# Two-layer block kernel: first half of the attention outputs turned and projected inside the last block

## The chip, the cores and the metric

One core of one Trainium2 chip. A core has TensorE (matmul; "PE" in the profile, its weight loads "PEld"), VectorE ("DVE"), ScalarE ("ACT"), GpSimd ("POOL") and SyncE ("SP"), which issues the transfers. Each engine runs its own instructions in the order of the program and meets the others by semaphores. The metric is the time of one execution on the device, in microseconds (us).

## What is computed

A block of four stages over 1024 tokens of width 256, each stage added to x behind a layer norm with learned shifts, scales and gates. Stage 1 is a linear attention, stage 2 a feed-forward part with 4-bit weights, stage 3 a masked softmax attention, stage 4 a feed-forward part of width 1024 whose gate has a low-rank term made from a second softmax attention. Cut to what the change touches:

```python
# stage 3: x = x + ga * _L1_attn_ref(h, ...)
att = jnp.where(causal, jnp.einsum('bhqd,bhkd->bhqk', q, k) / scale, -jnp.inf)   # 16 heads of width 16
y = jnp.einsum('bhqk,bhkd->bhqd', jax.nn.softmax(att, axis=-1), v)
y = jnp.einsum('bte,fe->btf', y.transpose(0, 2, 1, 3).reshape(b, t, e), Wo) + bo
# stage 4: x = x + gb * _L1_ffn_ref(h, ...)
attn = _attention(_rmsnorm(hidden_states, ln1_w), Wq, Wk, Wv, Wo)   # the same kind of attention
mod = MOD_SCALE * jnp.tanh(attn @ A)                                # A: 256 x 16
h = _rmsnorm(residual, ln2_w)
gate_pre = h @ W_in_base.T + mod * (h @ A) @ B
mlp_out = jax.nn.silu(gate_pre) * (h @ W_up_base.T) @ W_down.T
return residual + mlp_out
```

## The kernel before

The program is written out engine by engine, with counting semaphores; there is no scheduler at build time except one planner for the attention. x stands in SBUF with tokens on the partitions (8 tiles of 128 tokens). Projections want the channels on the partitions, so TensorE turns tiles of 128 x 128 (a "transpose" is a matmul against the identity `ident`), four to a PSUM bank; the eight banks hold 512 float32 values per partition each. "Half 0" is the first 512 tokens, "half 1" the other 512.

The softmax attention is run twice, `attention(0)` for stage 3 and `attention(1)` for stage 4 ("layer 0" and "layer 1" below). It works in 8 blocks: blocks 0 to 3 are four groups of heads over the queries of half 0, blocks 4 to 7 the same groups over the queries of half 1. For each block TensorE makes the scores once for their row maxima ("max", L750, taken by VectorE at L1303), and then again as transposed scores ("score", L776 with the mask L779) in steps of 128 keys; ScalarE takes the exponential of each pair of score banks (L972); TensorE multiplies with the values ("value", L790) into bank 3. At a block's end ScalarE copies bank 3 to SBUF ("copy", L990), TensorE turns it ("out", L799), and VectorE divides by the sum (L1322, L1324) into `att`, which has tokens on the partitions. A planner, `attention_order`, puts these pieces into one list `ORDER`, and TensorE, ScalarE and VectorE each walk through it. Steps 40 to 47 belong to block 7; step 44 is the first of its four masked steps. Block 3's sums, the last of half 0, are divided long before block 7 starts, block 6's during its first steps.

Behind `attention(0)` TensorE turns `att` (`attention_transposes`, L499, 16 transposes), ScalarE copies the four banks to `hT` (`attention_out`, L910), TensorE multiplies with the output weights (`out_projection`, L508, four units u of half and output channels, two matmuls each over kc, float32), ScalarE scales each unit (`projected`, L920), TensorE turns the result back in four quarters v (`update`, L521), VectorE adds each to x (L1226) and goes on with the norm of stage 4.

Behind `attention(1)` TensorE turns `att` (16 transposes, ScalarE's copies at L912), makes h times A for both halves (low-rank input; 12 matmuls, L463 to L465), then the attention outputs times the product of Wo and A (low-rank output; 4 float32 matmuls, L865). ScalarE takes the tanh (L1092), VectorE multiplies the two (three operations a half, from L1518). The feed-forward part `mlp(1)` begins with h times the first weights. Its weights are loaded by SyncE once all scores are done; ScalarE makes their high parts (`mlp_weights_hi`, L1002) and VectorE the low parts (`mlp_weights_lo`, L1368). GpSimd has the subtraction L1621 in each of its units.

## Time and profile before

| | us |
|---|---|
| median of 3 runs | 710.5 |
| lowest, highest | 709.95, 713.21 |
| the profiled execution, its own time | 709.6 |
| its span, first to last instruction | 707.9 |

| engine | busy us | share of the span |
|---|---|---|
| TensorE, matmuls | 654.1 | 92% |
| TensorE, weight loads | 407.0 | 58% |
| VectorE | 457.4 | 65% |
| ScalarE | 334.6 | 47% |
| GpSimd | 150.3 | 21% |

Matmuls overlap in the records (each row runs until its result is out), so a busy TensorE is not one at its peak, and the start of the next row tells more of the pace than a duration. A float32 matmul leaves two records. A row "x4" stands for four instructions in a stretch. In square brackets stands the idle time of the engine before the row and what ended it. The layer 0 attention runs from about 280 to 428 us, its output stage to 440, the layer 1 attention from about 470 to 619, and the feed-forward part from 629 to 701.

### The profile page before, as it was taken

Reading aid. Unit: us, or ns where it says so; the run is one execution under the profiler, and the core shown is the slowest. Engines: PE = TensorE matmul, PEld = TensorE weight load, DVE = VectorE, ACT = ScalarE, POOL = GpSimd, SP = SyncE. Lnnn points to the kernel's source line nnn. Section 1 sums busy time; section 2 is a strip of 40 time slices with the busy share of each in tenths; the row PEclk is TensorE's granted clock in tenths of the full one; section 3 lists DMA queues with packets and bytes.
Section 4 is the critical chain, followed back from the end, with each engine's and each line's share of the span. In section 5 each row is a group of like instructions: output and inputs, shape, how many; then the busy total and the mean of one; then the engine's idle time right before and its main releaser. Section 6 shows DMA issues by size and latency. Waiting matters only on the chain.

```text
span 707.9 us, 10654 instructions
## 1 busy us (share of the span) xinstructions
PE 654.1 (92%) x3959; PEld 407.0 (58%) x3965; DVE 457.4 (65%) x970; ACT 334.6 (47%) x531; POOL 150.3 (21%) x194
## 2 busy tenths in 40 slices
PE   4999989999999879799999998898899999999996
PEld 3666657777777746355444435484454444368884
DVE  5658787777777288778888602548688887242223
ACT  5325243333333423345566684562464657843332
POOL 3001224555555701310000000031100001002331
PEclk9999799999999999989999999999999999999999
DMA  8602410000000003566000000075540000050001
GB/s 270 219 0 91 120 53 0 24 22 23 1 0 1 0 1 91 132 183 135 2 2 2 2 1 1 0 177 149 122 93 2 2 2 3 16 164 1 0 1 59
DMA packets 36415, 38.34 MB, mean 54 GB/s; under 512 B 4034, under 2 KB 35292, under 8 KB 36108
## 3 DMA queue, kind: packets, MB, share of 16 engines
q1 hardware_dynamic: 36364, 37.67, 19.5%
q8 instruction: 31, 0.51, 0.3%
q14 instruction: 20, 0.16, 0.1%
HBM read 30.11 MB, written 7.34 MB: 53 GB/s over the span
## 4 chain that ended last, share of the span: by engine, by line
PE 50%; issue 22%; POOL 11%; DVE 9%; ACT 3%; SPq 2%; DMA 1%; POOLq 0%; DVEq 0%; ACTq 0%
POOL it_lo L1621 9%; PE psum L790 9%; PE psum L750 8%; PE psum L776 7%; PE psum L463 4%; PE psum L464 3%; PE psum L465 3%; POOL wd L1600 2%; DVE m L1303 2%; PE psum L508 2%; PE psum L779 2%; PE psum L753 2%; PE psum L579 2%; DVE mx L1303 1%; DVE x L1226 1%
## 5 line engine op out<-in xcount | busy, mean ns | idle before, releaser
L972 ACT ACTIVATE pt<-psum 128x1024 f32<-128x1024 f32 (+1 forms) x192 | 148.2, 811 | 94.4 <-PE psum L779 62.8
L1303 DVE TENSOR_REDUCE mx<-psum 128x1 f32<-128x512 f32 (+3 forms) x216 | 132.4, 664 | 16.4 <-PE psum L750 8.4
L750 PE MATMUL psum<-kr,qr 96*128 96x512 bf16 (+3 forms) x384 | 110.7, 338 | 10.3 <-DVE m L1303 5.2
L776 PE MATMUL psum<-qr,kr 99*128 99x512 bf16 (+3 forms) x384 | 99.2, 332 | 1.5 <-ACT pt L972 1.3
L1621 POOL TENSOR_TENSOR it_lo<-it,it_hi 128x512 fp32r<-128x512 f32 x48 | 67.2, 1401 | 146.9 <-ACT it_hi L1016 145.3
L790 PE MATMUL psum<-pt,vp 128*32 128x512 f32 (+3 forms) x768 | 82.1, 500 | 0.0
L750 PEld LDWEIGHTS psum<-kr,qr 96*128 96x128 bf16 x384 | 36.9, 100 | 73.7 <-DVE mx L1303 29.4
L463 PE MATMUL psum<-h_hi,wf_hi 128*128 128x512 f32 x192 | 75.5, 393 | 0.1
L1016 ACT CAST it_hi<-it 128x512 fp32r<-128x512 f32 x48 | 29.9, 622 | 95.6 <-DVE it L1380 95.6
L464 PE MATMUL psum<-h_lo,wf_hi 128*128 128x512 f32 x192 | 74.9, 390 | 0.0
L465 PE MATMUL psum<-h_hi,wf_lo 128*128 128x512 f32 x192 | 74.9, 390 | 0.0
L1303 DVE TENSOR_REDUCE m<-psum 128x1 f32<-128x384 f32 (+3 forms) x88 | 50.8, 634 | 21.7 <-PE psum L753 21.4
L1380 DVE TENSOR_TENSOR it<-psum,gl 128x512 f32<-128x512 f32 x48 | 32.8, 684 | 43.1 <-PE psum L465 39.6
L776 PEld LDWEIGHTS psum<-qr,kr 99*128 99x128 bf16 x384 | 35.8, 99 | 41.5 <-ACT pt L972 23.0
L779 PE MATMUL psum<-identb,tri 128*128 128x128 bf16 x256 | 51.3, 223 | 0.0
L753 PE MATMUL psum<-tri,identb 128*128 128x128 bf16 x256 | 51.2, 228 | 0.0
L1651 POOL TENSOR_SCALAR m<-m 128x16 bf16<-128x16 f32 x16 | 4.0, 253 | 220.6 <-DVE m L1309 153.9
L463 PE MATMUL psum<-it_hi,wf_hi 128*128 128x512 f32 x96 | 39.5, 411 | 7.2 <-POOL it_lo L1621 7.2
L463 PEld LDWEIGHTS psum<-h_hi,wf_hi 128*128 128x128 f32 x192 | 36.1, 188 | 8.5 <-issue 0.8
L464 PEld LDWEIGHTS psum<-h_lo,wf_hi 128*128 128x128 f32 x192 | 36.1, 188 | 7.7 <-issue 0.2
L465 PEld LDWEIGHTS psum<-h_hi,wf_lo 128*128 128x128 f32 x192 | 36.1, 188 | 7.7
L1012 ACT ACTIVATE gl<-psum 128x512 f32<-128x512 f32 x48 | 28.6, 596 | 24.3 <-PE psum L542 16.4
(201 smaller groups left out, 1082.7 us busy)
## 6 DMA issues: line engine op xcount, KB each, us to landing
parts_scratch<-parts SPq DMA_DIRECT2D x12, 384.0 KB, 3.9
qr<-parts_scratch SPq DMA_DIRECT2D x16, 192.0 KB, 3.1
kr<-parts_scratch SPq DMA_DIRECT2D x16, 192.0 KB, 3.7
qr<-parts_scratch SPq DMA_DIRECT2D x16, 128.0 KB, 3.2
kr<-parts_scratch SPq DMA_DIRECT2D x16, 128.0 KB, 3.6
wmod<-in_L_wmod SPq DMA_DIRECT2D x1, 1536.0 KB, 6.1
parts_scratch<-qr SPq DMA_DIRECT2D x4, 384.0 KB, 4.7
x<-in_L_attn_x SPq DMA_DIRECT2D x2, 512.0 KB, 4.0
```

Source lines behind the costliest of these rows:

```text
L463: pe.matmul(dst, st_hi, mv_hi, start=first, stop=False)
L464: pe.matmul(dst, st_hi, mv_lo, start=False, stop=False)
L465: return pe.matmul(dst, st_lo, mv_hi, start=False, stop=last)
L750: m = pe.matmul(b, qr[0:PARTS_ROWS, c, h, (qt - 4 * c) * P:(qt - 4 * c + 1) * P], kr[0:PARTS_ROWS, ch, h, 0:w], start=True, stop=not diag)
L753: m = pe.matmul(b[:, w - P:w], identb[:, :], tri[:, :], start=False, stop=True)
L776: m = pe.matmul(bank[4 + 2 * at[0] + j][:, 0:w], kr[0:PARTS_ROWS + 3, kt // 4, h, (kt % 4) * P:(kt % 4 + 1) * P], qr[0:PARTS_ROWS + 3, c, ...
L779: m = pe.matmul(bank[4 + 2 * at[0] + j][:, 0:P], tri[:, :], identb[:, :], start=False, stop=True)
L790: m = pe.matmul(bank[3][32 * j:32 * j + 32, q0 - c * HALF:q0 - c * HALF + w], vp[:, kt, 4 * gp + j, :], pt[:, (n + j // 2) % 4, j % 2, 0:w ...
L972: act.activation(pt[:, n % 4, :, 0:w], psum[:, b:b + 2, 0:w], ACT.Exp, scale=0.25).then_inc(S["ex"], 1)
L1303: dve.tensor_reduce(dst, bank[at[0]][:, 0:k * w].rearrange("p (k w) -> p k w", k=k), AX, ALU.max).then_inc(S["p1_mx"], 1)
L1380: dve.tensor_tensor(it[:, N % 2, :], bank[5][:, :], gl[:, N % 2, :], ALU.mult).then_inc(S["it_s"], 1)
L1621: pool.tensor_tensor(it_lo[:, N % 2, :], it[:, N % 2, :], it_hi[:, N % 2, :].bitcast(F32), ALU.subtract).then_inc(S["it_l"], 1)
```

## The change

In both layers, the eight transposes of half 0 move from behind the attention into block 7, behind the second score pair of step 44 (`AHEAD = 44`), and ScalarE's two copies of them behind the exponentials of that step. They use banks 0 and 1; half 1 stays behind the attention and uses banks 6 and 7.

In layer 0 the output projection is split. The first matmul of unit 0 stands ahead of block 7's "out" transposes, where TensorE waits for ScalarE's copy of the sums; the second stands behind them, where it waits for VectorE. Then come the transposes of half 1, units 1 and 2, the transposes of x for quarters 0 and 1, unit 3, and quarters 2 and 3.

In layer 1 the low-rank output of half 0 stands ahead of the "out" transposes, the low-rank input of half 0 behind them, then the transposes of half 1, the low-rank input and the low-rank output of half 1. ScalarE takes the tanh of half 0 first, VectorE has the three operations of half 0 ahead of the low parts of the first weights. No instruction is added or taken away on any engine.

```diff
+AHEAD = 44
+        def att_bank(k, half, dt):
+            return ((6, 7, 0, 1) if k == 0 else (0, 1, 6, 7))[2 * half + dt]
+        def wo_bank(k, u):
+            return ((2, 3, 4, 5) if k == 0 else (0, 1, 4, 5))[u]
...
+            def out_projection(k, u, kcs=range(KC)):
+                half, dt = divmod(u, 2)
+                pe.wait_ge(S["at_e"], 4 * k + 2 * half + 2)
+                for kc in kcs:
+                    m = pe.matmul(bank[wo_bank(k, u)][:, :], woT[k][:, kc, dt * P:(dt + 1) * P],
+                                  attT[k][:, kc, half * HALF:(half + 1) * HALF],
+                                  start=kc == 0, stop=kc == KC - 1)
+                if kc == KC - 1:
                     m.then_inc(S["wo_m"], 1)
...
+            def low_rank_out(half):
+                pe.wait_ge(S["at_e"], 8 + 2 * half + 2)
+                for kc in range(KC):
+                    m = pe.matmul(bank[(4, 2)[half]][0:96, :], woa[:, kc, :],
+                                  attT[2][:, kc, half * HALF:(half + 1) * HALF], start=kc == 0, stop=kc == KC - 1)
+                m.then_inc(S["z_m"], 1)
+
+            def low_rank_in(half):
+                pe.wait_ge(S["h_ok"], 2 * half + 2)
...
                         m.then_inc(S["s2"], 1)
+                        if i == AHEAD and at[0] == 1:
+                            pe.wait_ge(S["att_w"], 8 * (l + 1) + 7)
+                            attention_transposes(l + 1, 0)
...
                     elif what == "out":
                         n = 8 * l + i
+                        if n == 7:
+                            out_projection(1, 0, (0,))
+                        elif n == 15:
+                            low_rank_out(0)
                         pe.wait_ge(S["ob"], n + 1)
...
             attention(0)
-            attention_transposes(1)
-            out_projection(1)
-            update(2)
+            out_projection(1, 0, (1,))
+            attention_transposes(1, 1)
+            out_projection(1, 1)
+            out_projection(1, 2)
+            update(2, 0, 2)
+            out_projection(1, 3)
+            update(2, 2, 4)
...
             attention(1)
-            attention_transposes(2)
-            pe.wait_ge(S["at_e"], 12)
             pe.wait_ge(S["ab"], 2)
...
+            low_rank_in(0)
+            attention_transposes(2, 1)
+            low_rank_in(1)
+            low_rank_out(1)
+            pe.wait_ge(S["z_ok"], 1)
             pe.wait_ge(S["bst"], 2)
             mlp(1)
...
+                        if i == AHEAD and at[0] == 1:
+                            attention_out(l + 1, 0)
...
+            def low_rank_tanh(half):
+                act.wait_ge(S["z_m"], half + 1)
+                act.activation(t1[0:96, half, :], bank[(4, 2)[half]][0:96, :], ACT.Tanh).then_inc(S["z_ok"], 1)
...
             attention(0)
-            attention_out(1)
-            projected(1)
+            projected(1, 0, 1)
+            attention_out(1, 1)
+            projected(1, 1, 4)
...
             attention(1)
-            attention_out(2)
+            low_rank_tanh(0)
+            attention_out(2, 1)
             mlp_weights_hi(1, 0)
-            for half in range(2):
-                act.wait_ge(S["z_m"], half + 1)
-                act.activation(t1[0:96, half, :], bank[2 + half][0:96, :], ACT.Tanh).then_inc(S["z_ok"], 1)
+            low_rank_tanh(1)
             mlp(1, ACT.Silu)
...
             attention(1)
-            mlp_weights_lo(1, 0)
 
             for half in range(2):
+                if half:
+                    mlp_weights_lo(1, 0)
                 dve.wait_ge(S["ha_m"], half + 1)
```

TensorE in layer 0, from the last value products (`pt`, `vp`) of block 7 to the fillers ahead of the norm (`spin`), before; `t` is the copy of the sums, `xn` with `ident` the transposes of `att` and then of the projected outputs, `hT,woT` the output projection:

```order
L790 MATMUL psum<-pt,vp 32x256 x4
L790 MATMUL psum<-pt,vp 32x128 x4
L799 MATMUL psum<-ident,t 128x128 x4
L499 MATMUL psum<-ident,xn 128x128 x16
L508 MATMUL psum<-hT,woT 128x512 x8
L521 MATMUL psum<-ident,xn 128x128 x16
L812 MATMUL psum<-a_rep,raw 128x96 x4
L480 MATMUL psum<-spin,identb 128x512 x18
```

and now:

```order
L818 MATMUL psum<-pt,vp 32x256 x4
L818 MATMUL psum<-pt,vp 32x128 x4
L515 MATMUL psum<-hT,woT 128x512
L831 MATMUL psum<-ident,t 128x128 x4
L515 MATMUL psum<-hT,woT 128x512
L507 MATMUL psum<-ident,xn 128x128 x8
L515 MATMUL psum<-hT,woT 128x512 x4
L529 MATMUL psum<-ident,xn 128x128 x8
L515 MATMUL psum<-hT,woT 128x512 x2
L529 MATMUL psum<-ident,xn 128x128 x8
L848 MATMUL psum<-a_rep,raw 128x96 x4
L489 MATMUL psum<-spin,identb 128x512 x18
```

Eight transposes are gone from here, a matmul of the projection stands on either side of the transposes of the sums, and the turning back is in two parts. The eight stand in step 44, ahead of the value product of step 43:

```order
L801 MATMUL psum<-qr,kr 128x512
L804 MATMUL psum<-identb,tri 128x128
L507 MATMUL psum<-ident,xn 128x128 x8
L818 MATMUL psum<-pt,vp 32x512 x4
L801 MATMUL psum<-qr,kr 128x384
```

where the scores (`qr,kr`) and mask (`tri`) of step 44 were followed by the value product at once. ScalarE in layer 1, from step 44's exponentials (`pt`) to the first of the feed-forward part (`gl`), before, with the semaphores that each row waits for:

```order
L972 ACTIVATE pt<-psum 128x1024 [waits pv,s2] x2
L972 ACTIVATE pt<-psum 128x2x384 [waits pv,s2] x2
L972 ACTIVATE pt<-psum 128x2x256 [waits pv,s2] x2
L972 ACTIVATE pt<-psum 128x2x128 [waits pv,s2] x2
L990 COPY t<-psum 128x512 [waits ot,pv]
L912 COPY attT<-psum 128x512 [waits att_t] x4
L1002 CAST wf_hi<-nat 128x768 [waits nat0,fdn]
L1092 ACTIVATE t<-psum 96x512 [waits z_m] x2
```

and now:

```order
L996 ACTIVATE pt<-psum 128x1024 [waits pv,s2] x2
L936 COPY attT<-psum 128x512 [waits att_t] x2
L996 ACTIVATE pt<-psum 128x2x384 [waits pv,s2] x2
L996 ACTIVATE pt<-psum 128x2x256 [waits pv,s2] x2
L996 ACTIVATE pt<-psum 128x2x128 [waits pv,s2] x2
L1016 COPY t<-psum 128x512 [waits ot,pv]
L1032 ACTIVATE t<-psum 96x512 [waits z_m]
L936 COPY attT<-psum 128x512 [waits att_t] x2
L1028 CAST wf_hi<-nat 128x768 [waits nat0,fdn]
L1032 ACTIVATE t<-psum 96x512 [waits z_m]
```

Two of the four copies stand ahead of step 45's exponentials, and one tanh ahead of the other two copies.

## Rows read from the trace of the kernel before

**Rows 1.** The page, the chain that ended last, shares of the span by engine.

```profile
PE 50%; issue 22%; POOL 11%; DVE 9%; ACT 3%; SPq 2%; DMA 1%; POOLq 0%; DVEq 0%; ACTq 0%
```

**Rows 2.** Timeline, layer 0, steps 44 and 45: start, us, engine, line, operation, [idle before].

```profile
419.33 1.94 ACT L972 ACTIVATE pt<-psum 128x1024 f32<-128x1024 f32 x2 [0.38 <-PE psum L779]
...
420.77 0.10 PEld L776 LDWEIGHTS psum<-qr,kr 99*128 99x128 bf16 x1 [0.84 <-ACT pt L972]
...
421.32 0.10 PEld L776 LDWEIGHTS psum<-qr,kr 99*128 99x128 bf16 x1 [0.21 <-ACT pt L972]
...
421.43 1.51 ACT L972 ACTIVATE pt<-psum 128x768 f32<-128x768 f32 x2 [0.16 <-PE psum L779]
```

**Rows 3.** Timeline, layer 0, from the last value product to the norm's transposes.

```profile
425.59 0.16 PEld L790 LDWEIGHTS psum<-pt,vp 128*32 128x32 f32 x8 [0.43 <-ACT pt L972]
...
426.72 0.42 PEld L799 LDWEIGHTS psum<-ident,t 128*128 128x128 f32 x4 [0.97 <-ACT t L990]
...
428.25 1.73 PEld L499 LDWEIGHTS psum<-ident,xn 128*128 128x128 f32 x16 [1.11 <-issue]
...
428.94 2.42 ACT L910 ACTIVATE hT<-psum,vec 128x512 f32<-128x512 f32 x4 [2.27 <-PE psum L499]
...
430.26 7.13 PE L508 MATMUL psum<-hT,woT 128*128 128x512 f32 x16
...
432.34 0.78 ACT L920 ACTIVATE xn<-psum,gbo,gate 128x512 f32<-128x512 f32 x1 [0.98 <-PE psum L508]
...
437.43 0.78 ACT L920 ACTIVATE xn<-psum,gbo,gate 128x512 f32<-128x512 f32 x1 [0.94 <-PE psum L508]
...
439.81 0.67 DVE L1226 TENSOR_TENSOR x<-psum,x 128x512 f32<-128x512 f32 x1
...
445.74 1.09 PE L472 MATMUL psum<-ident,xn 128*128 128x128 f32 x8 [0.40 <-DVE xn L1134]
```

**Rows 4.** Timeline, layer 1, from the last value product to the feed-forward part.

```profile
617.70 0.16 PEld L790 LDWEIGHTS psum<-pt,vp 128*32 128x32 f32 x8 [0.43 <-ACT pt L972]
...
618.83 0.42 PEld L799 LDWEIGHTS psum<-ident,t 128*128 128x128 f32 x4 [0.97 <-ACT t L990]
...
620.36 1.73 PEld L499 LDWEIGHTS psum<-ident,xn 128*128 128x128 f32 x16 [1.11 <-issue]
...
621.05 2.05 ACT L912 COPY attT<-psum 128x512 f32<-128x512 f32 x4 [2.27 <-PE psum L499]
...
623.16 0.16 PEld L463 LDWEIGHTS psum<-h_hi,a_hi 128*96 128x96 f32 x1 [1.07 <-ACT attT L912]
...
625.79 0.39 PE L465 MATMUL psum<-h_hi,a_lo 128*96 128x512 f32 x1
...
629.45 0.19 PEld L464 LDWEIGHTS psum<-h_lo,wf_hi 128*128 128x128 f32 x1 [0.24 <-issue]
```

**Rows 5.** Timeline, layer 1, the split of the weights and the low-rank product.

```profile
622.97 0.87 ACT L1002 CAST wf_hi<-nat 128x768 fp32r<-128x768 f32 x1
...
623.96 0.96 DVE L1368 TENSOR_TENSOR wf_lo<-nat,wf_hi 128x768 fp32r<-128x768 f32 x1 [3.72 <-ACT wf_hi L1002]
...
628.63 0.68 DVE L1518 SCALAR_TENSOR_TENSOR t<-t,psum 96x512 f32<-96x512 f32 x1 [3.71 <-ACT t L1092]
...
629.81 0.68 DVE L1524 TENSOR_TENSOR m_hi<-t,m_hi 32x512 fp32r<-32x512 f32 x1
...
634.13 1.29 POOL L1621 TENSOR_TENSOR it_lo<-it,it_hi 128x512 fp32r<-128x512 f32 x1 [38.26 <-ACT it_hi L1016]
...
634.92 1.32 DVE L1368 TENSOR_TENSOR wf_lo<-nat,wf_hi 128x768 fp32r<-128x768 f32 x1 [1.52 <-ACT wf_hi L1002]
```

**Rows 6.** Busy time by stretch: from:to, length, engines' busy (count), PEclk granted, DMA.

```profile
300.00:304.00 4.00, 4.00 (x21) 2.24 (x20) 3.97 (x7) 0.00 (x0) 0.33 (x2) 0.50 0.60 145
...
500.00:504.00 4.00, 4.00 (x33) 2.19 (x31) 2.19 (x4) 1.19 (x2) 0.00 (x0) 0.67 0.90 177
...
638.00:696.00 58.00, 58.00 (x256) 47.85 (x255) 16.25 (x19) 21.46 (x33) 17.61 (x14) 1.00 0.00 1
```

More of the change, by code:

```diff
@@ L492, in token_major, with attention_transposes, update @@
                 return m
-            def attention_transposes(k):
-                for u in range(4):
-                    half, dt = divmod(u, 2)
-                    pe.wait_ge(S["att_w"], 8 * k + (4 * half + 4 if k == 0 else 8))
+            def attention_transposes(k, half):
+                for dt in range(KC):
+                    pe.wait_ge(S["att_w"], 8 * k + (4 * half + 4 if k == 0 or half == 0 else 8))
                     for j in range(4):
-                        m = pe.transpose(bank[(6, 7, 0, 1)[u]][:, j * P:(j + 1) * P],
+                        m = pe.transpose(bank[att_bank(k, half, dt)][:, j * P:(j + 1) * P],
                                          att[:, 4 * half + j, dt * P:(dt + 1) * P], ident[:, :])
                     m.then_inc(S["att_t"], 1)
-            def out_projection(k):
-                for u in range(4):
-                    half, dt = divmod(u, 2)
-                    pe.wait_ge(S["at_e"], 4 * k + 2 * half + 2)
-                    for kc in range(KC):
-                        m = pe.matmul(bank[2 + u][:, :], woT[k][:, kc, dt * P:(dt + 1) * P],
-                                      attT[k][:, kc, half * HALF:(half + 1) * HALF],
-                                      start=kc == 0, stop=kc == KC - 1)
+            def out_projection(k, u, kcs=range(KC)):
[6 more added lines that the diff above has]
+                if kc == KC - 1:
                     m.then_inc(S["wo_m"], 1)
-            def update(r):
-                for v in range(4):
+            def update(r, first=0, last=4):
+                for v in range(first, last):
                     pe.wait_ge(S["ysem"], 4 * r + 2 * (v // 2) + 2)
@@ L669, in _ @@
             pe.wait_ge(S["mod_cp"], 3)
-            attention_transposes(0)
+            attention_transposes(0, 0)
+            attention_transposes(0, 1)
             pe.wait_ge(S["ca"], 8)
             pe.wait_ge(S["wt_hi"], 5)
-            out_projection(0)
+            for u in range(4):
+                out_projection(0, u)
             update(0)
@@ L716, in _ @@
             spread_transposes(1)
+            def low_rank_out(half):
[6 more added lines that the diff above has]
+                pe.wait_ge(S["h_ok"], 2 * half + 2)
+                tok = slice(half * HALF, (half + 1) * HALF)
+                for kc in range(KC):
+                    m = mm3(bank[half][0:96, :], a_hi[:, kc, :], a_lo[:, kc, :], h_hi[:, kc, tok], h_lo[:, kc, tok],
+                            kc == 0, kc == KC - 1)
+                m.then_inc(S["ha_m"], 1)
             def attention(l):
@@ L901, in layer_norm_mod, with attention_out @@
                                    bias=mod[:, l, 6 * second + dt:6 * second + dt + 1]).then_inc(S["ln_f"], 1)
[L903 to L907 removed]
+            def attention_out(k, half):
+                for dt in range(KC):
+                    act.wait_ge(S["att_t"], 4 * k + 2 * half + dt + 1)
+                    b, dst = bank[att_bank(k, half, dt)], attT[k][:, dt, half * HALF:(half + 1) * HALF]
                     if k == 1:
@@ L913, in attention_out, with projected @@
                     q.then_inc(S["at_e"], 1)
-            def projected(k):
+            def projected(k, first=0, last=4):
                 act.wait_ge(S["mod_ok"], k + 2)
-                for u in range(4):
+                for u in range(first, last):
                     half, dt = divmod(u, 2)
                     act.wait_ge(S["wo_m"], 4 * k + u + 1)
-                    act.activation(y[:, dt, half * HALF:(half + 1) * HALF], bank[2 + u][:, :], ACT.Identity,
+                    act.activation(y[:, dt, half * HALF:(half + 1) * HALF], bank[wo_bank(k, u)][:, :], ACT.Identity,
                                    scale=gate[:, k, 4 + dt:5 + dt], bias=gbo[:, k, dt:dt + 1]).then_inc(S["ysem"], 1)
@@ L1087, in _ @@
             attention(1)
-            attention_out(2)
+            low_rank_tanh(0)
+            attention_out(2, 1)
             mlp_weights_hi(1, 0)
-            for half in range(2):
-                act.wait_ge(S["z_m"], half + 1)
-                act.activation(t1[0:96, half, :], bank[2 + half][0:96, :], ACT.Tanh).then_inc(S["z_ok"], 1)
+            low_rank_tanh(1)
             mlp(1, ACT.Silu)
```

20 lines of the change are left out of this document (2 added, 18 removed).

## Prediction

> **What bounds the kernel now.** I read three views: the chain of work that ended last, then the timeline around the two places that the change touches (the end of each masked attention), then the busy time and granted clock by stretches. The chain [rows 1] gives TensorE half of the span, and 22% to "issue", time in which nothing shown released the engine. So the kernel is mostly TensorE in program order, and what can be won is TensorE time on the path, or a wait of TensorE that ends last. The timeline at the end of layer 0's attention [rows 3] shows two such waits in a row: 0.9 us for ScalarE's copy of the last sums and 1.1 us for VectorE to divide them. Layer 1 has the same two, and then 1.07 us for ScalarE's copy of the turned outputs [rows 4]. Behind layer 1's end comes the feed-forward part, where TensorE is busy 58.00 of 58.00 us [rows 6], so that time won ahead of it reaches the end of the kernel. Behind layer 0's end comes the norm, a chain of VectorE and ScalarE for which TensorE waits (the last row of [rows 3]): there a gain counts from the moment at which VectorE gets its last additions of x.
>
> **Cost inside the last block, both layers.** Behind score step 44 stand 8 transposes more. 16 of them load in 1.73 us [rows 3], so 8 take 0.86 on TensorE. Queued behind them are the value product of step 43 and the scores of step 45; ScalarE's exponentials wait for these. ScalarE gets two copies: 4 took 2.42 in layer 0 [rows 3] and 2.05 in layer 1 [rows 4], so 1.21 and 1.03, queued ahead of the exponentials of step 45. Who is held? In layer 0 the two exponentials of step 44 run from 419.33 to 421.27 [rows 2], the copies then to 422.48. TensorE, which began the scores of step 45 at 420.77 and released an exponential 0.66 later [rows 2], begins at 421.63 and releases it at 422.29. It starts at 422.48 instead of 421.43, 1.05 later; but TensorE had been held by ScalarE once here (0.21) and ScalarE by TensorE (0.16), and these take back a part. Followed step by step with the durations of the trace, the last value product starts 0.8 us later in layer 0, and a little less in layer 1, whose copies are shorter. I take **0.8 and 0.8**. Bounds: 0.65 each if the 0.21 is all slack, and 2.07 and 1.89 if transposes and copies lay one behind the other on the path. The transposes wait for the divided sums of block 6 as well; by the program's order these are made some steps before, so that wait has ended.
>
> **Layer 0's tail** (times without the 0.8). The last value product ends at 425.59 plus 0.21, the four transposes of the sums start at 426.72 [rows 3]: 0.92 us. The first matmul of the output projection goes in there. A unit of the projection is two such matmuls, and ScalarE took unit 0 at 432.34 and unit 3 at 437.43 [rows 3], so a unit is 1.70 and a matmul 0.85: it fits, and costs nothing (0.1 if the switch costs). Its partner fills the wait for VectorE (transposes done at 427.15, next ones at 428.25): nothing. Then 8 transposes instead of 16, from 428.28 to 429.14. Units 1 and 2 of the projection, 1.70 each, to 432.6. ScalarE scales unit 0 first (0.78, from 428.4) and then copies twice (1.21), to 430.4, and unit 2 begins after that, at 430.9. Transposes of x's first half, 0.86, to 433.5; unit 3 to 435.2. ScalarE begins on a unit 0.38 after its end (432.34 less 430.26 and 1.70) and takes 0.78: 436.4. Transposes at 436.4, VectorE 0.7 behind a transpose's start (428.25 against 428.94 for ScalarE): VectorE's third addition of x starts at 437.1, in place of 439.81 [rows 3]. **2.7 us earlier.** From there on the same operations of VectorE follow in the same order. The filler matmuls ahead of the norm's transposes end 2.4 earlier and left 0.40 us of waiting (the last row of [rows 3]), so that 0.1 is left: nothing of the gain is lost there. Net of the block: **1.9 us**.
>
> **Layer 1's tail.** From 617.91 (617.70 plus 0.21) to the feed-forward part, whose second product loads at 629.45 [rows 4], are 11.5 us. In it TensorE has 20 transposes (2.16), 12 products of the low-rank input (the first at 623.16, the twelfth at 625.79: 0.24 each, 2.87) and 4 of the low-rank output at 0.85 (3.40): 8.4. The rest is the waits, 0.9, 1.1 and 1.0. Afterwards: 12 transposes (1.30), 2.87 and 3.40, sum 7.6, with 0.2 for changing between kinds of matmul 7.8. Are the waits really filled? The low-rank output of the first half (1.70) is longer than the 0.9 that it fills, and pushes the transposes of the sums back by 0.8. Behind their start VectorE needs 1.53 (618.83 to 620.36), TensorE has 0.43 and 1.43 of work: filled. ScalarE's two copies are done 1.7 after the start of the turning (621.05 less 620.36, and half of 2.05); TensorE has 0.86 and 1.43: filled. So 11.5 less 7.8, **3.7 us**; of these 0.8 come back in the block. The weights' low parts now stand behind the three VectorE operations of the first half, which take 1.86 (628.63 to 630.49 [rows 5]): these run from about 621.8 to 623.7, ScalarE's high parts (0.87) end at 624.2, the low parts (0.96 [rows 5]) at 625.2, and TensorE wants them at 625.3. That is no cushion, so I charge **0.1**. Net **2.8 us**. The loads of the weights start behind the last scores, as before, and ScalarE, which did not wait for the first one [rows 5], wants it 0.3 later than now. The branch for layer 0's first, linear attention is the same order with other names: nothing.
>
> **A rule of the skill.** The low parts took 0.96 with GpSimd idle, and 1.32 when GpSimd's subtraction ran from 634.13 to 635.42 and they were issued at 634.92 [rows 5]. The Trainium skill, "SBUF — State Buffer", section "SBUF: two separate sides", has VectorE (two inputs in SBUF) and GpSimd lock a shared port pair for a whole instruction, and the trace agrees: the end at 636.24 is 0.8 behind GpSimd's. By that rule the moved operation keeps its 0.96, since GpSimd has nothing until the first product is there, and the charge is 0.1. By the longer row alone, without the rule, it would be 0.4.
>
> **The sum.** 1.9 and 2.8 are 4.7 us. The profiled execution took 709.6 (span 707.9), which would be 704.9. The median of the runs is 710.5, 0.9 above: **705.8 us**, 0.66% less. What a measurement of this kernel can tell from no change is about 0.5%, 3.55 us, so the forecast lies only a little beyond it.
>
> **Rivals.**
> - *The block pays in full.* For: in these steps TensorE and ScalarE release each other in turn, and 0.16 to 0.2 is all the slack there is. Against: the copies start when step 44's exponentials are done, while TensorE is already at the value product. Price: 3.96 in place of 1.6. Time 708.2, within 0.5%. Chance 0.13.
> - *The weights become the wait.* ScalarE's and VectorE's split of the first weights ends after the low-rank products. With 1.32 and a late start, 0.4 to 0.9 us of TensorE waiting for VectorE just ahead of the feed-forward part. Time 706.5. Chance 0.12.
> - *Layer 0's gain stays in layer 0.* The second layer's scores wait for transfers through memory; if something there, or a filler, were last at a fixed time, 1.9 would go. Against: these transfers are issued by work that moves along. Time 707.7. Chance 0.10. That the change does not do what it says I rule out for the order of TensorE, which is as described; it would show up as this case.
> - *The clock, slower than before.* At the start of an attention TensorE waits and the granted clock falls to its lower level, 1.2 GHz: 0.67 on average from 500 to 504, 0.50 from 300 to 304 [rows 6]. A stretch at the lower level costs half its length if TensorE is the bound. The change moves the following work against whatever decides when the level returns. It eats the gain from 9.4 us of more low clock on, and makes the kernel 0.5% slower than before from 16.5 on; 18 us would give 714.8. For: the level does differ between the two layers at the same work. Against: no row shows it low for over four microseconds behind the start of dense work. Chance 0.05.
>
> **The numbers.** Forecast 0.60, faster by over 0.5% with the weights' case: 0.72. Within 0.5%: the full price and the lost layer 0, 0.23. Slower 0.05. Range: down to 704.3 (the block at 0.65 each, seamless fills, and the charge for the weights gone, 0.8 less, and as much for the scatter of runs), up to 708.5, which takes in the first and third rival and leaves out the clock.
>
> **What would show it.** Right: no wait of TensorE over 0.2 us between the last value product and the feed-forward part in layer 1, that stretch 7.8 us long, and some 4.7 us of waits gone there and in layer 0; VectorE's third addition of x 11.5 us behind the last value product of layer 0, in place of 14.2; the last value product some 7.0 us after the exponentials of step 44 start, in place of 6.3 in layer 0. Wrong: exponentials of step 45 over 1.3 us later against those of step 44 (full price); VectorE's low parts named as what the feed-forward part waits for; a granted clock below 1 for long behind the second layer's first scores.

## The result and the profile after

| | us |
|---|---|
| changed kernel, median of 20 runs | 706.21 (703.91 to 711.61) |
| kernel before, median of 20 runs in the same session | 711.22 (707.97 to 714.70) |
| ratio of the two, 95% interval | 0.993 (0.991 to 0.995) |
| forecast | 705.8 (704.3 to 708.5), ratio 0.9934 |

The change makes the kernel faster by 0.7%, 5.0 us. Each layer's edit takes the waits away that it was meant to take, at the price forecast. In the traces half of layer 0's net gain goes again at the start of the second attention; whether it does so in most executions stays open.

The profiled execution alone would say the opposite. The page of the changed kernel begins with:

```profile
span 709.9 us, 10657 instructions
...
PE 50%; issue 22%; POOL 11%; DVE 9%; ACT 3%; DMA 2%; SPq 1%; POOLq 0%; DVEq 0%; ACTq 0%
```

That is 2.0 us more than the 707.9 of before, and the chain's shares are those of [rows 1], except that DMA and SyncE's queue have changed places. But this execution (711.6 us) is the longest of its 20, and the loss lies ahead of anything that the change touches: the exponentials of step 44 in layer 0 start at 425.21, against 419.33 in [rows 2], 5.88 later behind the same instructions. In a second profiled execution of the same kernel, with a span of 703.7, the last value product of layer 0 starts at 426.25 in place of 432.25. What can be compared is the part behind step 44: 709.9 less 425.21 is 284.7 us, against 707.9 less 419.33, 288.6. **3.9 us less** in this pair of executions.

**Inside the block.** The timeline of the changed kernel, layer 0, steps 44 and 45 (start, us, engine, line, operation, idle before), answers [rows 2]:

```profile
425.21 1.94 ACT L996 ACTIVATE pt<-psum 128x1024 f32<-128x1024 f32 x2 [0.38 <-PE psum L804]
...
425.51 0.86 PEld L507 LDWEIGHTS psum<-ident,xn 128*128 128x128 f32 x8
...
427.04 1.27 ACT L934 ACTIVATE hT<-psum,vec 128x512 f32<-128x512 f32 x2
...
427.54 0.10 PEld L801 LDWEIGHTS psum<-qr,kr 99*128 99x128 bf16 x1 [0.84 <-ACT pt L996]
...
428.19 1.52 ACT L996 ACTIVATE pt<-psum 128x768 f32<-128x768 f32 x2
```

The eight transposes take 0.86 and two copies 1.27. TensorE's scores of step 45 start 2.33 behind the exponentials of step 44 (before 1.44), so they are pushed back by 0.89, and the next exponentials start 2.98 behind them instead of 2.10.

**Behind the block, layer 0**, answering [rows 3]:

```profile
432.25 0.16 PEld L818 LDWEIGHTS psum<-pt,vp 128*32 128x32 f32 x8 [0.43 <-ACT pt L996]
...
432.61 0.30 PEld L515 LDWEIGHTS psum<-hT,woT 128*128 128x128 f32 x2 [0.20 <-issue]
...
433.38 0.55 PEld L831 LDWEIGHTS psum<-ident,t 128*128 128x128 f32 x4 [0.48 <-ACT t L1016]
...
433.90 0.30 PEld L515 LDWEIGHTS psum<-hT,woT 128*128 128x128 f32 x2
...
442.98 1.09 PE L529 MATMUL psum<-ident,xn 128*128 128x128 f32 x8 [0.87 <-ACT xn L944]
...
443.67 0.69 DVE L1257 TENSOR_TENSOR x<-psum,x 128x512 f32<-128x512 f32 x1 [1.67 <-PE psum L529]
...
449.61 1.09 PE L481 MATMUL psum<-ident,xn 128*128 128x128 f32 x8 [0.21 <-DVE xn L1165]
```

The last value product is at 432.25; the first matmul of the projection (L515) lies in the first wait and leaves the transposes of the sums (L831) where they were, 1.13 behind it. The second follows them at once. VectorE's third addition of x comes 11.42 behind the last value product, before 14.22; the norm's transposes 17.36, before 20.15.

**Behind the block, layer 1**, answering [rows 4] and [rows 5]:

```profile
623.45 0.16 PEld L818 LDWEIGHTS psum<-pt,vp 128*32 128x32 f32 x8 [0.43 <-ACT pt L996]
623.80 0.24 PEld L732 LDWEIGHTS psum<-attT,woa 128*96 128x96 f32 x2 [0.20 <-issue]
...
625.17 0.14 PEld L831 LDWEIGHTS psum<-ident,t 128*128 128x128 f32 x1 [0.27 <-issue]
...
627.20 1.03 PEld L507 LDWEIGHTS psum<-ident,xn 128*128 128x128 f32 x8
...
629.03 0.85 ACT L1028 CAST wf_hi<-nat 128x768 fp32r<-128x768 f32 x1
...
630.00 0.96 DVE L1399 TENSOR_TENSOR wf_lo<-nat,wf_hi 128x768 fp32r<-128x768 f32 x1 [0.52 <-ACT wf_hi L1028]
...
631.19 0.19 PEld L472 LDWEIGHTS psum<-h_hi,wf_hi 128*128 128x128 f32 x1 [0.49 <-issue]
...
631.40 0.19 PEld L473 LDWEIGHTS psum<-h_lo,wf_hi 128*128 128x128 f32 x1
...
636.10 1.29 POOL L1653 TENSOR_TENSOR it_lo<-it,it_hi 128x512 fp32r<-128x512 f32 x1 [35.25 <-ACT it_hi L1046]
...
636.90 1.31 DVE L1399 TENSOR_TENSOR wf_lo<-nat,wf_hi 128x768 fp32r<-128x768 f32 x1 [1.53 <-ACT wf_hi L1028]
```

From 623.45 to the feed-forward part's second product at 631.40 are 7.95 us, before 11.75. The waits of 0.97, 1.11 and 1.07 in [rows 4] are gone; what is left between TensorE's loads there are gaps of 0.20 to 0.29 and one of 0.49, and its matmul rows follow on one another without a gap. The low-rank output (L732) is longer than the first wait and puts the sums' transposes 1.72 behind the last value product instead of 1.13.

**The start of the second attention.** This stretch holds the same instructions in both kernels, from its first scores to the transposes of its first sums. Before, rows of the timeline and a window over the stretch (length, busy us and count of PE, PEld, DVE, ACT and POOL, then the granted clock as a share of full speed, and the DMA columns):

```profile
477.81 0.10 PEld L750 LDWEIGHTS psum<-kr,qr 96*128 96x128 bf16 x1 [0.68 <-issue]
...
498.79 0.10 PEld L750 LDWEIGHTS psum<-kr,qr 96*128 96x128 bf16 x1 [3.38 <-ACT m3T L983]
...
511.38 0.42 PEld L799 LDWEIGHTS psum<-ident,t 128*128 128x128 f32 x4 [0.84 <-issue]
...
477.80:511.40 33.60, 28.95 (x220) 14.53 (x220) 25.08 (x44) 11.43 (x18) 2.82 (x12) 0.90 0.51 131
...
502.60:506.00 3.40, 3.40 (x46) 2.18 (x39) 2.56 (x6) 0.77 (x2) 0.94 (x4) 1.00 0.61 111
```

and after:

```profile
481.73 0.10 PEld L775 LDWEIGHTS psum<-kr,qr 96*128 96x128 bf16 x1 [0.68 <-issue]
...
502.36 0.10 PEld L775 LDWEIGHTS psum<-kr,qr 96*128 96x128 bf16 x1 [3.53 <-ACT m3T L1009]
...
516.37 0.42 PEld L831 LDWEIGHTS psum<-ident,t 128*128 128x128 f32 x4 [0.84 <-issue]
...
481.70:516.40 34.70, 30.04 (x220) 15.00 (x220) 25.25 (x44) 11.48 (x18) 2.82 (x12) 0.85 0.53 133
...
505.50:508.90 3.40, 3.40 (x22) 1.54 (x21) 1.45 (x3) 0.46 (x1) 0.14 (x1) 0.50 0.77 140
```

34.64 us in place of 33.57: 1.07 of layer 0's gain are lost here, with the granted clock at 0.85 on average instead of 0.90. The loss lies behind TensorE's longest wait in the stretch (3.38 and 3.53 us). That wait ends 20.98 us behind the first scores before and 20.63 after; from its end to the transposes of the sums are 12.59 us before and 14.01 after. Before, the clock is back at full speed from 502.60 on; in the changed kernel the lower level (1.2 GHz) lasts 3.4 us longer, the window from 505.50 at 0.50. Between layer 0's norm and these scores nothing changed (32.08 and 32.12 from the norm's transposes).

The account behind step 44, in us: layer 0's block +0.77 and tail -2.78; start of the second attention +1.07; layer 1's block +0.76 and tail -3.80. The sum is -3.98, and the spans gave -3.9. The four terms of the change alone are -5.05.

### The profile page after: what moved, and what is told of

Same layout as the page of the kernel before. It is cut to its first block, busy times and chain, and to the rows that moved or that the text cites. A ratio compares the mean times of both kernels' runs of the same rounds, so it can differ in the third digit from the quotient of the medians.

```text
span 709.9 us, 10657 instructions
## 1 busy us (share of the span) xinstructions
PE 656.4 (92%) x3959; PEld 408.9 (58%) x3965; DVE 457.8 (64%) x970; ACT 334.9 (47%) x531; POOL 149.6 (21%) x194
## 4 chain that ended last, share of the span: by engine, by line
PE 50%; issue 22%; POOL 11%; DVE 9%; ACT 3%; DMA 2%; SPq 1%; POOLq 0%; DVEq 0%; ACTq 0%
POOL it_lo L1653 9%; PE psum L818 9%; PE psum L775 9%; PE psum L801 7%; PE psum L472 4%; PE psum L473 3%; PE psum L474 3%; DVE m L1334 2%; POOL wd L1632 2%; PE psum L515 2%; PE psum L804 2%; PE psum L778 2%; PE psum L587 2%; DVE mx L1334 1%; PE psum L500 1%
```

## The experiments

A "block" below is the time from block 6's transposes of the sums to block 7's last value product (before 12.78 and 12.80 in the two layers, after 13.55 and 13.56); a "tail" runs from there to the norm's transposes (layer 0) or the feed-forward part's second product (layer 1). Where a median is given, the kernel before had its runs in the same session: 710.76 for the first four kernels of the table, 711.01 for the other two.

| kernel | median | ratio, 95% interval | layer 0: block, tail | start of 2nd attention | layer 1: block, tail | sum of the traces' differences |
|---|---|---|---|---|---|---|
| before | | | 12.78, 20.15 | 33.57 | 12.80, 11.75 | |
| changed kernel again | 705.71 | 0.9936 (0.9911 to 0.9961) | 13.55, 17.36 | 34.52 | 13.55, 7.97 | -4.1 |
| layer 0 alone, relaxed wait | 708.67 | 0.9991 (0.9960 to 1.0021) | 13.55, 17.36 | 34.57 | 12.80, 10.73 | -2.0 |
| layer 1 alone, relaxed wait | 706.51 | 0.9938 (0.9909 to 0.9966) | 12.77, 19.07 | 34.35 | 13.56, 7.97 | -3.3 |
| spread, with three edits | 705.56 | 0.9935 (0.9904 to 0.9966) | 13.41, 17.36 | 34.91 | 13.41, 7.97 | -4.0 |
| layer 0 alone, pure | 709.29 | 0.9983 (0.9956 to 1.0011) | 13.54, 17.37 | 34.64 | 12.79, 11.74 | -1.0 |
| turned in the wait | 707.65 | 0.9960 (0.9927 to 0.9992) | 12.77, 18.83 | 34.26 | 12.80, 9.79 | -2.6 |

### Each layer alone

The two layers' edits are separated by a pair of flags, `(1, 0)` in the first kernel and `(0, 1)` in the second:

```diff
+NEW = (1, 0)
...
-                        if i == AHEAD and at[0] == 1:
+                        if i == AHEAD and at[0] == 1 and NEW[l]:
...
+            if NEW[1]:
                 low_rank_in(0)
                 attention_transposes(2, 1)
                 low_rank_in(1)
                 low_rank_out(1)
+            else:
+                attention_transposes(2, 0)
+                attention_transposes(2, 1)
...
```

> The change in layer 0 alone; layer 1 as before. Theory: the two layers' gains are independent and reach the end, layer 0's being 2.78 us in the tail less 0.78 in the last block, 2.0 us: ratio about 0.997. In the trace the stretch from the last value product to the norm's transposes is 17.4 us in place of 20.1 and layer 1's tail is as before, 11.75 us. Rival (layer 0's gain stays in layer 0, because the second layer waits for its transfers at a fixed time): ratio 1.000, and the second attention's first scores come no earlier behind the norm.

> The change in layer 1 alone; layer 0 as before. Theory: 3.80 us in the tail less 0.77 in the last block, 3.0 us: ratio about 0.996; layer 1's tail 7.95 us in place of 11.75, layer 0's as before, 20.1 us. Rival (all of the gain is layer 1's): ratio 0.993, as the whole change.

The changed layer behaves in each as in the full change. The other layer surprised: its tail is 10.73 instead of 11.75 (layer 1) and 19.07 instead of 20.15 (layer 0). The reason is one line that the flags left as the change has it: the transposes of half 0 wait for that half's divisions, not for all eight. The loads of the first kernel in layer 1:

```profile
624.54 0.90 PEld L512 LDWEIGHTS psum<-ident,xn 128*128 128x128 f32 x8
...
625.62 0.85 PEld L512 LDWEIGHTS psum<-ident,xn 128*128 128x128 f32 x8 [0.18 <-DVE xn L1388]
```

Half 0's eight run directly behind the sums' transposes and fill VectorE's 1.11 us of dividing; only half 1's wait. One changed wait is worth 1.0 us a layer and costs the block nothing (12.80 and 12.77). It also means that these two kernels are no clean separation, so a third took the wait back.

```diff
-                    pe.wait_ge(S["att_w"], 8 * k + (4 * half + 4 if k == 0 or half == 0 else 8))
+                    pe.wait_ge(S["att_w"], 8 * k + (4 * half + 4 if k == 0 or (half == 0 and NEW[k - 1]) else 8))
```

> Layer 0 changed alone, and layer 1 as before in every respect, its turning's wait for the last divided sums included (the earlier kernel with layer 0 alone had layer 1's first eight transposes run ahead of it). In the trace: last value product of layer 0 13.55 us behind block 6's transposes of the sums, norm's transposes 17.36 behind that product (before: 12.8 and 20.14), layer 1 as before with 12.8 and 11.75. Theory that each layer's gain goes through to the end: 2.0 us less than before, ratio 0.9972. Rival that layer 0's gain is lost on the way to the end: ratio 1.000, and the stretch from layer 0's norm to layer 1's block longer by 2.0.

The trace shows all four stretches as expected, and besides them the start of the second attention at 34.64. With it the sum is 1.0 us, a ratio of 0.9986; measured 0.9983. The interval holds 0.9972 and 1.000 as well, so the ratio alone decides nothing. What speaks for a loss is that the traces repeat it: where layer 0's tail was 17.36 this stretch took 34.51 to 34.91 in seven profiled executions (clock 0.85 each time), and in those with the tail of before 33.57, 33.77, 31.94 and 34.32 (clock 0.90, 0.90, 0.89, 0.85). The last shows that it is no rule of layer 0's edit alone, and so do the three other traces: 34.35 with layer 1 alone, 34.26 with the turning in the wait (last experiment), 33.51 without the fills. What goes with the length of this stretch in all 14 traces stands in the last section.

The ratios of the two kernels with the relaxed wait did not come out as their theories had it. Layer 0 alone has 0.9991 (theory 0.997, rival 1.000) and layer 1 alone 0.9938 (theory 0.996, rival 0.993, all of the gain is layer 1's): both stand nearer the rival, and both intervals hold theory and rival.

### The price in the block

Three kernels put duplicates into the kernel before and leave all else where it was: eight transposes more behind step 44's scores (`DUP = 1`), ScalarE's two copies more (`COPIES = 2`), and 24 transposes (`DUP = 3`).

```diff
+                        if i == AHEAD and at[0] == 1 and DUP:
+                            pe.wait_ge(S["att_w"], 8 * (l + 1) + 7)
+                            for dt in (0, 1) * DUP:
+                                for j in range(4):
+                                    pe.transpose(bank[dt][:, j * P:(j + 1) * P], att[:, j, dt * P:(dt + 1) * P], ident[:, :])
...
+                        if i == AHEAD and at[0] == 1 and COPIES:
+                            act.wait_ge(S["att_w"], 8 * (l + 1) + 7)
+                            for dt in range(COPIES):
+                                act.copy(attT[l + 1][:, dt, 0:HALF], bank[dt][:, :])
```

> The kernel before with eight transposes of half 0 added behind step 44's scores (their results unused), no copies: the TensorE part of the price in the block alone. Theory (TensorE is the bound of the masked steps, with 0.1 us of slack): from the exponentials of step 44 to the last value product 7.0 us in both layers, in place of 6.26. Rival (full price only with the copies, TensorE has slack of its own): 6.5 us or less.

> The kernel before with ScalarE's two copies of 128x512 added behind step 44's exponentials, no transposes: the ScalarE part alone. Theory (both parts overlap, since the copies stand in the shadow of the transposes): also about 7.0 us by itself in layer 0, although the changed kernel with both has 7.04. Rival (ScalarE has slack in the masked steps and its copies are free): 6.3 us.

> The kernel before with three times the eight transposes at step 44, no copies. Theory: each further eight cost all of their 0.86 us on TensorE, so 6.26 plus 0.75 plus 1.72: 8.7 us from the exponentials of step 44 to the last value product. Rival (the slack between ScalarE and TensorE takes more up): under 8 us.

Of the first kernel's trace, layer 0's last exponentials of step 44, the eight transposes and the last value product:

```profile
420.46 1.94 ACT L978 ACTIVATE pt<-psum 128x1024 f32<-128x1024 f32 x2 [0.38 <-PE psum L780]
...
420.76 0.86 PEld L787 LDWEIGHTS psum<-ident,xn 128*128 128x128 f32 x8
...
427.49 0.16 PEld L796 LDWEIGHTS psum<-pt,vp 128*32 128x32 f32 x8 [0.43 <-ACT pt L978]
```

7.03 us from the first to the last, as in the changed kernel with the copies (7.04), against 6.26: the price is the transposes' alone. Sixteen more made it 8.78, that is 0.87 for each further eight: the full 0.86 of TensorE, and no slack left. The copies alone miss their expectation: 6.77 instead of about 7.0, 0.5 for 1.1 of ScalarE's time. So each engine's part has a price by itself, and together they cost no more than the larger. (These duplicates are plain copies, 1.08 for the two in layer 0. Layer 0's own copies add a bias and take 1.27; no run has those alone.) These three were run once (710.69, 716.23 and 719.24, beside 710.20 for the kernel before); the first four hundred microseconds scatter too much for such a time to be read, and the blocks are what counts. Whether ScalarE is free beside the transposes was tried by letting VectorE make the copies:

```diff
-                        if i == AHEAD and at[0] == 1:
-                            attention_out(l + 1, 0)
...
+                    elif what == "score" and i == AHEAD and at[0] == 1:
+                        for dt in range(KC):
+                            dve.wait_ge(S["att_t"], 4 * (l + 1) + dt + 1)
+                            dst = attT[l + 1][:, dt, 0:HALF]
...
```

> The changed kernel with VectorE making the two copies of half 0 in place of ScalarE, the transposes still in step 44. Theory (the copies stand in the shadow of the transposes): 7.0 us from the exponentials of step 44 to the last value product, 0.04 less than the changed kernel. Rival (the copies are what costs): 6.4 us.

The block is 13.55 in both layers, the tails 17.37 and 7.97, the time 705.89 (one run, beside 708.15 for the kernel before): nothing gained to speak of, as this theory had it. ScalarE in layer 0, step 45:

```profile
422.66 1.51 ACT L996 ACTIVATE pt<-psum 128x768 f32<-128x768 f32 x2 [1.04 <-PE psum L804]
```

ScalarE now waits 1.04 us for TensorE, and these exponentials still start 2.98 behind those of step 44 (419.68). It is 2.98 with ScalarE's copies, with VectorE's and with none, so TensorE's transposes alone set it.

### Is the gain in the filled waits?

The turning stays in the block, but no matmul stands in a wait:

```diff
-                        if n == 7:
-                            out_projection(1, 0, (0,))
-                        elif n == 15:
-                            low_rank_out(0)
...
-            low_rank_in(0)
             attention_transposes(2, 1)
+            low_rank_out(0)
+            low_rank_in(0)
             low_rank_in(1)
             low_rank_out(1)
```

> The changed kernel with half 0 still turned in step 44, but nothing in the waits for the sums' copy and for VectorE: in layer 0 both matmuls of unit 0 stand behind the transposes of half 1, in layer 1 the low-rank output and input of half 0 do. Theory (the gain is the filled waits): layer 0's tail 17.4 plus 1.7, 19.1 us; layer 1's 7.95 plus 2.0, 9.9 us. Rival (the gain is the transposes that are gone from the tail, and the fills are incidental): 17.4 and 8 us.

Tails of 19.01 and 10.07, near what was expected (707.17, one run). In layer 1:

```profile
618.09 0.42 PEld L827 LDWEIGHTS psum<-ident,t 128*128 128x128 f32 x4 [0.97 <-ACT t L1013]
619.62 0.86 PEld L507 LDWEIGHTS psum<-ident,xn 128*128 128x128 f32 x8 [1.11 <-issue]
```

Both waits are back, as long as in [rows 4]. Set against the block's price, turning early without the fills is worth 1.13 less 0.77, or 0.4 us, in layer 0, and 1.68 less 0.76, or 0.9, in layer 1; the fills bring 1.65 and 2.1. The relaxed wait of the section above, 1.0 us for nothing, is worth more than turning early without fills. No run relaxes that wait in both layers and changes nothing else.

### Do the first weights hold TensorE?

The high parts ahead of ScalarE's copies, so that VectorE has them sooner:

```diff
             low_rank_tanh(0)
-            attention_out(2, 1)
             mlp_weights_hi(1, 0)
+            attention_out(2, 1)
```

> The changed kernel with ScalarE's high parts of the first weights ahead of its copies of half 1. Theory (the low parts, ready at 630.96, held TensorE's first product of the feed-forward part by 0.2 us, and stood behind ScalarE's high parts, not behind VectorE's own three operations): layer 1's tail 7.75 us in place of 7.95, with no idle time of TensorE ahead of that product beyond the 0.24 to 0.27 of its weight loads. Rival (the first weights have not landed by then, and the high parts hold the copies up): 7.95 or more.

The tail is 7.97, not shorter. The rows of ScalarE, VectorE and TensorE:

```profile
621.89 0.83 ACT L1028 CAST wf_hi<-nat 128x768 fp32r<-128x768 f32 x1 [0.87 <-DMA nat<-in_L_ffn_W_down]
...
624.15 0.96 DVE L1399 TENSOR_TENSOR wf_lo<-nat,wf_hi 128x768 fp32r<-128x768 f32 x1
...
625.62 0.19 PEld L472 LDWEIGHTS psum<-h_hi,wf_hi 128*128 128x128 f32 x1 [0.27 <-issue]
```

ScalarE ran into the transfer of the weights (0.87 of waiting), yet the low parts are ready at 625.11, 0.5 ahead of the first product's load. That load comes 7.54 us behind the last value product (618.08) instead of 7.74, with 0.27 of idle time ahead of it instead of 0.49; so the late low parts may well have held it by 0.2, as the theory says. But the next load then waits 0.24 and comes at 7.97, where it came at 7.95: the 0.2 only changes places, and making the weights ready sooner wins nothing.

### Spread, and the variant in the wait

One kernel joins three edits: the eight transposes in two fours behind steps 42 and 43, VectorE's copies, and the weights first.

```diff
-AHEAD = 44
+AHEAD = 43
+AHEADS = (42, 43)
...
-                        if i == AHEAD and at[0] == 1:
+                        if i in AHEADS and at[0] == 1:
                             pe.wait_ge(S["att_w"], 8 * (l + 1) + 7)
-                            attention_transposes(l + 1, 0)
+                            attention_transposes(l + 1, 0, AHEADS.index(i))
```

> The changed kernel with three more edits: the eight transposes are spread over steps 42 and 43 (four each), VectorE makes the two copies in place of ScalarE, and ScalarE splits the first weights' high parts ahead of its copies of half 1. Theory: steps 42 and 43 are held by ScalarE, so the eight transposes (0.86 us of TensorE) cost 0.4 to 0.5 us a layer instead of 0.78, and the weights no longer hold TensorE by 0.2: 0.8 us less than the changed kernel, ratio to before 0.992. From the transposes of block 6's sums to the last value product 13.3 us in both layers (before 12.8, the changed kernel 13.55). Rival (transposes cost their full time wherever they stand): 13.6 us, and a ratio of 0.993.

The block takes 13.41 in each layer, 0.14 us less. Of the two other edits neither shortened anything alone, so this is the spreading's; it was to cost 0.4 to 0.5 and costs 0.63 and 0.61. The time was to be 0.8 us less, and 705.56 against 705.71 for the changed kernel again can't be told apart.

> The changed kernel itself, on the chip of the three others, for comparison: ratio 0.993, layer 0's tail 17.4 us, layer 1's 7.95, exponentials of step 44 to the last value product 7.04 in both layers.

The last kernel asks whether the block need be touched at all. Half 0 is turned in the 0.92 us ahead of the sums' transposes, and what filled the waits moves one place back.

```diff
-            return ((6, 7, 0, 1) if k == 0 else (0, 1, 6, 7))[2 * half + dt]
+            return ((6, 7, 0, 1) if k == 0 else (4, 5, 6, 7))[2 * half + dt]
...
-                        if n == 7:
-                            out_projection(1, 0, (0,))
-                        elif n == 15:
-                            low_rank_out(0)
+                        if i == 7:
+                            attention_transposes(l + 1, 0)
...
-            out_projection(1, 0, (1,))
+            out_projection(1, 0, (0,))
             attention_transposes(1, 1)
+            out_projection(1, 0, (1,))
```

> Nothing inside the block: the eight transposes of the first half stand where TensorE waits for ScalarE's copy of block 7's sums (0.92 of waiting, 0.86 of work), in banks 4 and 5, ScalarE copies them behind that copy; behind the transposes of the sums come the first matmul of the output projection (layer 0) and the low-rank input of the first half (layer 1), the projection's second matmul and the low-rank output of the first half stand behind the transposes of the second half. Theory that TensorE's work is only moved between bound stretches and that the gain is the filled waits alone: block 12.8 in both layers in place of 13.55, layer 1's tail 8.8 in place of 7.97, layer 0's 18.6 in place of 17.36, 4.5 us less than before in all, ratio 0.9937. Rival that turning inside the block wins something of its own: tails longer by more than 1.3 than in the changed kernel and ratio 0.996 or more.

The block is free, as expected, but layer 1's tail is 9.79 and not 8.8, and the ratio, 0.9960, stands at the rival's mark. First TensorE's wait for ScalarE's copies in layer 0, then VectorE's low parts and TensorE's first product in layer 1:

```profile
426.77 0.30 PEld L515 LDWEIGHTS psum<-hT,woT 128*128 128x128 f32 x2 [0.78 <-issue]
...
624.38 0.96 DVE L1395 TENSOR_TENSOR wf_lo<-nat,wf_hi 128x768 fp32r<-128x768 f32 x1
...
625.56 0.19 PEld L472 LDWEIGHTS psum<-h_hi,wf_hi 128*128 128x128 f32 x1 [1.55 <-ACT t L1027]
```

In layer 1 the tanh of half 0, and with it VectorE's three operations, come later, so that the low parts end at 625.34 and TensorE starts 0.22 behind them, after 1.55 of waiting, of which 0.27 is usual there. The row names ScalarE's second tanh (its end is at 625.49), but the first product needs only the first tanh by the program, and the low parts. This is the case "the weights become the wait", at a price of about 1 us. In layer 0 the copies of half 0 aren't ready when the sums' transposes are done: 0.78. So both marks of the rival came: the tails are 1.47 and 1.82 longer than in the changed kernel, and the ratio is 0.9960. What turning in the block wins, by these rows, is that its results are ready early enough for what has to follow.

## Why the prediction was right

- **The cost in the block**: 0.8 and 0.8 forecast, 0.77 and 0.76 measured. The way to it was another. The prediction has ScalarE's copies hold the exponentials of step 45 by 1.05 and 0.2 of that handed back. They came 0.88 later, with ScalarE's copies, with VectorE's and with none, and 0.1 was handed back: the price is that of the 0.86 of transposes on TensorE, which alone cost 0.77. That both ways end at 0.8 is in part luck. The rival that the block pays in full (3.96 for both layers) is refuted, with 1.53.
- **Layer 0's tail**: 2.7 forecast, 2.78 measured; VectorE's third addition 11.5 behind the last value product forecast, 11.42 measured. The fillers left 0.21 of waiting ahead of the norm's transposes (forecast 0.1, before 0.40), so they did not hold it.
- **Layer 1's tail**: 3.7 less the charge of 0.1 forecast, 3.80 measured. The charge was not needed: the low parts were ready at 630.96, 0.23 ahead of the product, and making them ready sooner did not shorten the tail. The sign "no wait of TensorE over 0.2 us" was not met to the letter (gaps of 0.27, 0.29 and 0.49 between loads), the length was: 7.95 from the start of the last value product, 7.74 as the prediction counts, for 7.8. Its "plus 0.21" for the end of that product is 0.16 in the row, which makes the first wait 0.97 and not 0.92 and changes nothing else. They took 0.96 with GpSimd idle. The next ones took 1.31 beside its subtraction and ended at 638.21, 0.82 behind the subtraction's end, as in [rows 5]; the rule of the Trainium skill in "SBUF — State Buffer", "SBUF: two separate sides", fits both.
- **The sum**: 4.7 forecast. The four terms measure 5.05, the medians differ by 5.0. The 0.35 between are 0.2 in layer 1's tail (half of it the charge that didn't come), 0.08 in layer 0's and 0.07 in the blocks.
- **Where it was incomplete**: the step "VectorE's operations follow in the same order, nothing of the gain is lost there" holds up to the second attention's scores, and no further. In the trace 1.07 us go between those scores and the first sums. Of the rivals, "layer 0's gain stays in layer 0" happened by half, and the way it happened is that of the clock's rival: 3.4 us more at the lower level, which cost 1.07, where it needed 9.4 us more to eat the gain. Its "against", that no row shows the level low for over four microseconds behind the start of dense work, does not hold in the changed kernel, where it lasted 6.8. For the medians this stays open, as the ratios show that the traces' sums would give (over 710.8 us) with this stretch's difference and without it:

| kernel | with | without | measured |
|---|---|---|---|
| changed | 0.9944 | 0.9929 | 0.9930 |
| changed, again | 0.9942 | 0.9929 | 0.9936 |
| layer 0 alone, relaxed wait | 0.9971 | 0.9957 | 0.9991 |
| layer 1 alone, relaxed wait | 0.9953 | 0.9942 | 0.9938 |
| spread | 0.9944 | 0.9925 | 0.9935 |
| layer 0 alone, pure | 0.9986 | 0.9971 | 0.9983 |
| turned in the wait | 0.9964 | 0.9954 | 0.9960 |

Both columns lie within the intervals, but for 0.9957 against the interval from 0.9960. One trace of before can't say how often its stretch takes 33.57.

## What to carry to other kernels

An engine that runs in program order and waits twice, for 0.9 and 1.1 us, can be given work there only if its inputs are ready by then; so look first for what could be ready, then price making it ready where the engine is the bound (here 0.8 us for 0.86 of transposes) against the waits it fills (1.65 and 2.1 us beyond the turning itself). Look also for waits that ask for more than the instruction behind them needs: one threshold of a semaphore held 1.0 us a layer. When executions scatter by 8 us and a change is worth 5, compare the traces from the last common instruction on, stretch by stretch, with the granted clock of each stretch beside it.

## What the hardware showed beyond this

**The granted clock can fall in the middle of the dense end.** In the kernel with 24 transposes in the block, the tail of layer 1 took 13.22 instead of 11.75. Its windows over the end of the attention (columns as above), and the load of the 16 transposes there:

```profile
625.00:628.00 3.00, 1.94 (x26) 0.89 (x23) 0.29 (x2) 1.24 (x3) 0.00 (x0) 1.00 0.49 136
628.00:632.00 4.00, 3.46 (x16) 3.27 (x16) 0.40 (x1) 1.75 (x3) 0.00 (x0) 0.57 0.84 268
...
628.51 3.27 PEld L500 LDWEIGHTS psum<-ident,xn 128*128 128x128 f32 x16 [1.11 <-issue]
```

TensorE had been busy for 1.94 of 3.00 us, then the clock was granted at 0.57, nearly all of it at the lower level of 1.2 GHz, and sixteen transposes took 3.27 us in place of 1.73. Layer 0 of the same execution, with the same waits, did not show it, nor did any other kernel here. In this one execution the tail with its two waits of 1 us cost 1.5 us more than it does elsewhere; what decides it was not found.

**The start of the second attention varies with identical instructions**, between 31.94 and 34.91 us over 14 profiled executions. The mean clock is no full account: 31.94 came with 0.89 and 34.35 with 0.90. Where the lower level falls is one. In every trace TensorE has one long wait in the stretch (2.08 to 4.56 us), and it ends 20.6 to 21.4 us behind the first scores, whatever the clock did ahead of it. What differs is how long the lower level lasts from the start of that wait on:

| lower level from the wait on | from the wait's end to the sums' transposes | whole stretch | executions |
|---|---|---|---|
| none | 11.00 | 31.94 | 1 (transposes alone in the block) |
| 3.4 | 12.56 to 12.59 | 33.51 to 33.77 | 3 (before, copies alone, no fills) |
| 6.8 | 13.48 to 14.01 | 34.26 to 34.91 | 10 (all others, the changed kernel twice) |

In the one of the first row the lower level lay ahead of the wait, all 6.8 us of it, and the wait took it up by being shorter; behind it the clock was at full speed (first scores at 479.75):

```profile
490.30:497.20 6.90, 6.88 (x36) 3.79 (x34) 5.02 (x9) 2.05 (x2) 0.94 (x4) 0.51 0.97 251
497.20:508.00 10.80, 9.63 (x92) 5.19 (x90) 6.97 (x12) 4.43 (x9) 0.94 (x4) 1.00 0.50 136
...
500.69 0.10 PEld L751 LDWEIGHTS psum<-kr,qr 96*128 96x128 bf16 x1 [2.08 <-ACT m3T L993]
```

So the time at the lower level ahead of the wait cost nothing here, and behind its start the first 3.4 us cost 1.6 and the next 3.4 another 0.9 to 1.5. What puts an execution into one row or another was not found. All seven with layer 0's full edit are in the last row, but so are three without it.
